# Score matmuls of the first attention: three 32-row products stacked into one 96-row product, fed by on-chip transfers

## What is computed

```
x = x + _L0_xattn_ref(_layernorm(x), ctx, ctx, Wq, bq, Wk, bk, Wv, bv, Wo, bo)
# 32 query heads of 16 features, 8 key/value heads, 4 query heads share one key head
# per batch: scores = q @ k.T / sqrt(16); softmax over the 128 context tokens; @ v; @ Wo + bo
```

## Time and profile before

| | us |
|---|---|
| median of 3 runs (lowest, highest) | 1848.16 (1847.71, 1848.89) |
| the profiled execution, its own time | 1848.91 |
| its span, first to last instruction | 1847.1 |
| the block of the first attention (84 to 262 us of the span) | 178 |
| PE busy over the whole span | 1687.6 (91%) |
| ACT busy over the whole span | 810.1 (44%) |

### The profile page before, as it was taken

The page is one execution under the profiler, slowest core; times in us unless marked ns, Lnnn a source line. Parts: engine busy times, 40 slices in busy tenths (PEclk is TensorE's granted clock), DMA queues, the critical chain, the costliest instruction groups (busy, mean ns, idle before and its releaser), DMA issues. The chain is left out here.

```text
span 1847.1 us, 27513 instructions
## 1 busy us (share of the span) xinstructions
PE 1687.6 (91%) x8898; PEld 1406.5 (76%) x8898; DVE 1205.1 (65%) x2393; ACT 810.1 (44%) x2591; POOL 1007.9 (55%) x1031
## 2 busy tenths in 40 slices
PE   3899967489999999999999999999999999997796
PEld 2777856368888888888788878888888888886684
DVE  5367665637777777766777775566655655554695
ACT  2088840134444444444344444444444444444342
POOL 2033320046666677766667676656656776662353
PEclk9989989599999999999999999999999999999896
DMA  3000010022222222221112222222222332220100
GB/s 132 24 1 1 0 40 1 26 68 64 69 58 64 69 69 77 67 57 58 52 57 59 62 80 75 58 69 75 63 67 72 90 93 70 79 75 6 59 18 29
DMA packets 57233, 104.10 MB, mean 56 GB/s; under 512 B 8016, under 2 KB 8528, under 8 KB 56976
## 3 DMA queue, kind: packets, MB, share of 16 engines
q1 hardware_dynamic: 55440, 99.27, 18.6%
q10 hardware_dynamic: 1664, 3.21, 0.5%
HBM read 100.36 MB, written 2.10 MB: 55 GB/s over the span
## 5 line engine op out<-in xcount | busy, mean ns | idle before, releaser
L891 POOL TENSOR_TENSOR a_probs<-a_probs,a_total 128x512 f32<-128x512 f32 x128 | 135.3, 1057 | 210.7 <-DVE a_total L1315 208.5
L83 POOL TENSOR_TENSOR a_w_lo<-a_raw,a_w_hi 128x512 fp32r<-128x512 f32 x186 | 240.5, 1293 | 14.9
L68 PE MATMUL ps<-a_wo_hi,a_oT_lo 128*128 128x512 f32 x544 | 225.1, 414 | 6.9 <-DVE a_oT_lo L83 5.4
L70 PE MATMUL ps<-a_wo_hi,a_oT_hi 128*128 128x512 f32 x544 | 213.7, 393 | 0.0
L69 PE MATMUL ps<-a_wo_lo,a_oT_hi 128*128 128x512 f32 x544 | 212.1, 390 | 0.0
L1152 ACT ACTIVATE a_v_hi<-ps 128x128 fp32r<-128x128 f32 x128 | 35.5, 278 | 359.3 <-PE ps L1000 359.3
L83 POOL TENSOR_TENSOR a_wo_lo<-a_raw,a_wo_hi 128x512 fp32r<-128x512 f32 x128 | 165.4, 1292 | 10.3
L1290 DVE TENSOR_TENSOR a_cross<-ps,a_cross 128x512 f32<-128x512 f32 x128 | 88.2, 689 | 120.1 <-ACT a_cross L1138 117.6
L1299 DVE SCALAR_TENSOR_TENSOR a_probs<-a_cross,a_q_scale,a_mask 128x128 f32<-128x128 f32 x256 | 156.4, 670 | 0.0
L83 DVE TENSOR_TENSOR a_pT_lo<-ps,a_pT_hi 128x512 fp32r<-128x512 f32 x192 | 128.4, 682 | 25.7 <-ACT a_pT_hi L2093 20.1
L1993 POOL TENSOR_TENSOR a_probs<-a_probs,a_total 128x1024 f32<-128x1024 f32 x32 | 60.8, 1899 | 153.5 <-DVE a_total L2149 153.5
(11 more groups left out here) (408 smaller groups left out, 5031.5 us busy)
## 6 DMA issues: line engine op xcount, KB each, us to landing
a_raw<-in_L_wq SPq DMA_DIRECT2D x128, 256.0 KB, 2.7
a_raw<-in_L_wo SPq DMA_DIRECT2D x128, 256.0 KB, 2.6
a_raw<-in_L_wkv SPq DMA_DIRECT2D x64, 256.0 KB, 2.6
a_raw<-in_L_main SPq DMA_DIRECT2D x12, 256.0 KB, 3.1
setup_raw<-in_cT SPq DMA_DIRECT2D x4, 512.0 KB, 7.1
x<-in_x ACTq DMA_DIRECT2D x8, 256.0 KB, 9.0
t_c_raw<-in_context SPq DMA_DIRECT2D x8, 256.0 KB, 5.7
out<-x SPq DMA_DIRECT2D x8, 256.0 KB, 2.0
```

The lines of the kernel that those rows point to most:

```text
L68: pe.matmul(out, lhs_lo, rhs_hi, start=start, stop=False)
L70: return pe.matmul(out, lhs_hi, rhs_hi, start=False, stop=stop)
L83: return eng.tensor_tensor(out_lo, value, hi.bitcast(F32), ALU.subtract)
L891: pool.tensor_tensor(heads(probs[:, :]), heads(probs[:, :]), along_last(total[:, :], S), ALU.mult).then_inc(s["probs"], 1)
```

## The change

PE's three 32-row matmuls of a set become one matmul of 96 rows. The operands are laid one under another: rows 0 to 31 hold `q_hi` and `k_hi`, rows 32 to 63 `q_lo` and `k_hi`, rows 64 to 95 `q_hi` and `k_lo` (of the four heads' rows that belong to the round). The contraction over 96 rows then sums the three products. `scores` issues 4 matmuls a round instead of 12.

Engines write only the partitions that they read, so the stacks `q_stack` and `k_stack` are filled by DMA transfers within the on-chip memory: six a round (64 KB each for q, 32 KB for k), 24 a batch, 192 in all, every one issued by SP. SP waits for the `lo` parts of the batch, and for the scores of the batch two before (which read the same stack). `scores` waits for its own round's six transfers, by one of eight new semaphores. `stage_qk` on ACT no longer waits for scores but for all 24 transfers of the batch two before, which read the buffers that it writes. q and k are now staged two batches ahead: batch 1 before the first round, and batch i+2 in step (i, 0).

```
+PAIR = 2 * HD0
+        q_stack = [ph.sb(f"q_stack{p}", ROUNDS * SETS * S, F32R, 3 * PAIR) for p in (0, 1)]
+        k_stack = [ph.sb(f"k_stack{p}", ROUNDS * 2 * S, F32R, 3 * PAIR) for p in (0, 1)]
+        STACKED = 16 * 3
@@ block.sync
+            def stack(i, p):
+                sp.wait_ge(s["q_lo"], i + 1)
+                sp.wait_ge(s["k_lo"], 2 * (i + 1))
+                wait_from_one(sp, s["s_mm"], ROUNDS * (i - 1))
+                for r in range(ROUNDS):
+                    rows = slice(PAIR * r, PAIR * r + PAIR)
+                    for n, (q, k) in enumerate(((0, 0), (1, 0), (0, 1))):
+                        to = slice(PAIR * n, PAIR * n + PAIR)
+                        sp.dma_start(q_stack[p][to, blk(r, SETS * S)].bitcast(F32), q_s[p][q][rows, :].bitcast(F32)).then_inc(s[f"stacked{p}{r}"], 16)
+                        sp.dma_start(k_stack[p][to, blk(r, 2 * S)].bitcast(F32), k_s[p][k][rows, :].bitcast(F32)).then_inc(s[f"stacked{p}{r}"], 16)
+            for i in range(B):
+                stack(i, i % 2)
@@ block.tensor, scores
-                if r == 0:
-                    pe.wait_ge(s["q_lo"], i + 1)
-                    pe.wait_ge(s["k_lo"], 2 * (i + 1))
+                pe.wait_ge(s[f"stacked{p}{r}"], STACKED * (i + 2 - p))
...
-                    last = matmul_split(pe, bank_s[r % 2][:, n * 2 * S:(n + 1) * 2 * S],
-                                        tuple(x[rows, n * S:(n + 1) * S] for x in q_s[p]),
-                                        tuple(x[rows, :] for x in k_s[p]), True, True)
+                    last = pe.matmul(bank_s[r % 2][:, n * 2 * S:(n + 1) * 2 * S], q_stack[p][:, blk(r * SETS + n, S)],
+                                     k_stack[p][:, blk(r, 2 * S)], start=True, stop=True)
@@ block.scalar, stage_qk
-                wait_from_one(act, s["s_mm"], ROUNDS * (i - 1))
+                for r in range(ROUNDS):
+                    wait_from_one(act, s[f"stacked{p}{r}"], STACKED * (i - p))
@@ block.scalar, and the same on block.vector
             stage_qk(0, 0)
+            stage_qk(1, 1)
...
-                if r == 0 and exists(i + 1):
-                    stage_qk(i + 1, 1 - p)
+                if r == 0 and exists(i + 2):
+                    stage_qk(i + 2, p)
```

More of the change, by code:

```diff
@@ L1956, in attention_small_heads @@
         raw_max, neg_max, total = ([ph.sb(f"{n}{p}", RH) for p in (0, 1)] for n in ("raw_max", "neg_max", "total"))
+        q_stack = [ph.sb(f"q_stack{p}", ROUNDS * SETS * S, F32R, 3 * PAIR) for p in (0, 1)]
+        k_stack = [ph.sb(f"k_stack{p}", ROUNDS * 2 * S, F32R, 3 * PAIR) for p in (0, 1)]
         oT, keep = ph.split("oT", SETS * S), ph.sb("keep", 2)
-        s = ph.sems("wo_in wo_hi wo_lo keep zeroed q_hi q_lo k_hi k_lo v_hi v_lo s_mm raw_max neg_max exped inverse probs"
+        s = ph.sems("wo_in wo_hi wo_lo keep zeroed q_hi q_lo k_hi k_lo stacked00 stacked01 stacked02 stacked03 stacked10 stacked11 stacked12 stacked13 v_hi v_lo s_mm raw_max neg_max exped inverse probs"
                     " pT_mm pT_hi pT_lo av_mm oT_hi oT_lo o_mm added")
@@ L2004, in scores @@
                 R = i * ROUNDS + r
-                if r == 0:
-                    pe.wait_ge(s["q_lo"], i + 1)
-                    pe.wait_ge(s["k_lo"], 2 * (i + 1))
+                pe.wait_ge(s[f"stacked{p}{r}"], STACKED * (i + 2 - p))
                 wait_from_one(pe, s["exped"], RH * (R - 1))
-                rows = slice(32 * r, 32 * r + 32)
                 for n in range(SETS):
-                    last = matmul_split(pe, bank_s[r % 2][:, n * 2 * S:(n + 1) * 2 * S],
-                                        tuple(x[rows, n * S:(n + 1) * S] for x in q_s[p]),
-                                        tuple(x[rows, :] for x in k_s[p]), True, True)
+                    last = pe.matmul(bank_s[r % 2][:, n * 2 * S:(n + 1) * 2 * S], q_stack[p][:, blk(r * SETS + n, S)],
+                                     k_stack[p][:, blk(r, 2 * S)], start=True, stop=True)
                 last.then_inc(s["s_mm"], 1)
```

## The result

| | before | after |
|---|---|---|
| median of 20 executions each, us | 1848.87 | 1853.41 |
| lowest and highest | 1846.93, 1853.41 | 1850.44, 1855.76 |
| profiled execution / its span | 1848.91 / 1847.1 | 1853.84 / 1852.1 |
| mean granted clock of PE in it | 0.958 | 0.949 |

The ratio after to before is 1.0020, 95% interval 1.0013 to 1.0026. The forecast was 1843.2, range 1836.5 to 1850.5: the time lies outside it, and the change costs time instead of giving 5 us. None of the 20 executions after is under 1850.4 us; 12 of the 20 before are under 1849.

A forecast was written before the change was run, and what follows sets the result against it. PE bounds the first attention's block, ACT close behind. Waits -6.3 and -1.3, staging -1.1, start +1.0, clock falls -1.6 and +4.3 sum to -5.0 us: profiled 1848.91 becomes 1843.9, median 1843.2; range 1836.5 to 1850.5.

## What to carry to other kernels

Where a change moves work ahead of a loop, count the issues of its queue up to the first consumer and to whoever must wait for the last one, at the pace of that very shape, and give half of the transfers to an engine that is idle there. Where a saving lengthens the part of a batch in which PE does little, reckon that its clock falls there, and weigh a few useless matmuls in that place, which cost nothing at full clock while another engine is the bound. And take more than one profile of the kernel before: if its times fall in groups with different mean clocks, an effect under the distance of the groups can't be read from two traces.

## What was not expected of the hardware

- A transfer within the chip from 32 to 32 rows (32 or 64 KB) takes SP 0.59 us, 0.63 from one to the next, where the loads of the earlier trace rows took 0.47; the same transfer issued by GpSimd takes 0.50. From issue to landing it is 1.9 to 2.0 us.
- Going from matmuls of 128 rows to matmuls of 32 and back cost PE 0.4 us a round here, on top of the matmuls themselves (0.32 and 0.33 us at the two steps that otherwise take 0.23, and the rest within the scores). At 96 rows it does not occur.
- One VectorE subtraction of 128x512 took 2.21 us beside a GpSimd multiplication of 1.90 us, and 0.69 without one.
- Delaying everything behind the block by 2.4 us cost 5.2 us in one kernel and 0 in the other.
- Falls of the clock in the same places of unchanged code come and go between executions of one kernel; a pair of them costs 2 to 4 us. What sets them is open.
